# Causal attention, top-2 experts and combining in one block, with all result loads issued at once

## What is computed

```python
x = x + _L0_xattn_ref(_layernorm(x), ctx, ctx, ...)      # 16 heads of 8
x = x + _L0_ffn_ref(_layernorm(x), gate_w, expert_w)     # the best of 8 experts
x = x + _L1_xattn_ref(_layernorm(x), ctx, ctx, ...)      # the same, causal
x = x + _L1_ffn_ref(_layernorm(x), ...)

def _L1_ffn_ref(x, router_w, gate_proj, up_proj, down_proj):   # F = 352
    probs = softmax(x @ router_w)
    routing_weights, routing_idx = top_k(probs, 2)             # of 8, then normalised to sum 1
    # for each of a token's two experts e:
    #   y_e = (silu(x @ gate_proj[e]) * (x @ up_proj[e])) @ down_proj[e]
    return sum over both of weight_e * y_e
```

## Time and profile before

| | us |
|---|---|
| three timed runs | 892.91, 894.95, 895.14 (median 894.95) |
| the profiled execution, its own time | 895.08 |
| its span, first to last instruction | 893.3 |
| mean granted TensorE clock, share of full | 0.879 |
| TensorE busy | 670.4 (75% of the span) |
| VectorE, ScalarE, GpSimd busy | 483.9 (54%), 385.5 (43%), 347.6 (39%) |

### The profile page before, as it was taken

The page is one execution under the profiler, slowest core; times in us unless marked ns, Lnnn a source line. Parts: engine busy times, 40 slices in busy tenths (PEclk is TensorE's granted clock), DMA queues, the critical chain, the costliest instruction groups (busy, mean ns, idle before and its releaser), DMA issues. The chain is left out here.

```text
span 893.3 us, 21719 instructions
## 1 busy us (share of the span) xinstructions
PE 670.4 (75%) x7687; PEld 458.0 (51%) x7717; DVE 483.9 (54%) x1275; ACT 385.5 (43%) x948; POOL 347.6 (39%) x506
## 2 busy tenths in 40 slices
PE   1566648898996898994499999998406999999910
PEld 1343326676774454541155666665304877787700
DVE  1687446676772677773356888887341222222213
ACT  0344325575774012121056666667303665666500
POOL 4354240010011134342034477778841544455410
PEclk9988677899998899997589999999556999999965
DMA  3459831464302999999014333300111222212027
GB/s 95 132 152 182 209 114 24 80 108 81 74 3 38 208 239 209 216 219 228 7 23 77 72 90 87 84 26 26 43 36 48 59 55 61 58 55 64 28 72 222
DMA packets 93273, 87.17 MB, mean 98 GB/s; under 512 B 7785, under 2 KB 87921, under 8 KB 90097
## 3 DMA queue, kind: packets, MB, share of 16 engines
q1 hardware_dynamic: 84592, 74.70, 38.9%
q0 software_dynamic: 4352, 8.99, 3.2%
q10 hardware_dynamic: 4224, 2.10, 0.8%
HBM read 43.99 MB, written 41.76 MB: 96 GB/s over the span
## 5 line engine op out<-in xcount | busy, mean ns | idle before, releaser
L861 DVE TENSOR_REDUCE nm<-bank 128x8 f32<-128x1024 f32 x128 | 156.5, 1223 | 63.8 <-PE bank L633 61.7
L763 ACT ACTIVATE pr<-bank 128x512 f32<-128x512 f32 x256 | 147.2, 604 | 85.0 <-PE bank L657 82.2
L1572 DVE TENSOR_TENSOR exac<-bank,exsi 128x352 f32<-128x352 f32 x72 | 37.8, 525 | 127.8 <-PE bank L1479 121.0
L1029 POOL TENSOR_SCALAR_AFFINE_SELECT pr<-pr 128x1024 f32<-128x1024 f32 x64 | 69.7, 1088 | 75.3 <-ACT pr L763 75.1
L1451 POOL DMA_INDIRECT results<-exy,exre x72 | 70.8, 983 | 33.0 <-issue 33.0
L670 PE MATMUL bank<-pr,values 128*9 128x128 f32 x2048 | 82.3, 280 | 1.7 <-POOL pr L1029 1.7
L654 PE MATMUL bank<-qq,kk 48*128 48x128 bf16 x1024 | 76.8, 223 | 6.4 <-issue 4.2
L1308 PE MATMUL bank<-e0ch,expert_w 128*128 128x512 f32 x128 | 71.9, 644 | 8.2 <-DVE e0ch L1220 8.1
L657 PE MATMUL bank<-mt,pick 64*128 64x128 bf16 x1024 | 76.8, 223 | 0.0
L633 PE MATMUL bank<-kk,qq 48*128 48x128 bf16 x1024 | 55.5, 233 | 19.5 <-DVE nm L861 8.0
L1058 POOL DMA_INDIRECT sorted_in<-rrrow,rrpli x64 | 63.2, 988 | 14.2 <-issue 14.0
(11 more groups left out here) (203 smaller groups left out, 1304.3 us busy)
## 6 DMA issues: line engine op xcount, KB each, us to landing
sorted_in<-padding SPq DMA_DIRECT2D x8, 2145.0 KB
k_parts<-pj_parts SPq DMA_DIRECT2D x16, 384.0 KB, 2.9
kk<-k_parts SPq DMA_DIRECT2D x32, 192.0 KB
qq<-q_parts SPq DMA_DIRECT2D x32, 192.0 KB
exx<-sorted_in SPq DMA_DIRECT2D x72, 65.0 KB
kk<-k_parts SPq DMA_DIRECT2D x32, 128.0 KB
qq<-q_parts SPq DMA_DIRECT2D x32, 128.0 KB
coy<-results SPq DMA_DIRECT2D x8, 512.0 KB, 4.7
```

Of the source, the lines that this page charges most:

```text
L763: act.activation(probs[c], st_bank[(n * NC + c) % ST][:], ACT.Exp, scale=scale).then_inc(exp_s, 1)
L861: dve.tensor_reduce(neg_max[n % 2][:, u * 2 * C4:(u + 1) * 2 * C4], s_pair.rearrange("q (h k) -> q h k", k=T), AX_X, ALU.max, negate=True) ...
L1029: pool.affine_select(out=probs_pair[u][:], in_=probs_pair[u][:], compare_op=ALU.is_ge, fill=0.0, base=0, pattern=[[0, 2 * C4], [1, T]], ch ...
```

## The change

1. `attention`, `run_experts` and `combine` no longer open a block each: they hand back a `Stage` of five functions, and one block calls the three stages' functions one after the other on each engine. The branches, the barriers and the clearing between attention(1) and the experts, and the block end between the experts and `combine`, are gone. In their place SP waits for the scatters of rows and for `tile_row` (semaphore `listed`) before its first load, TensorE for the readers of the PSUM banks that it takes over, and SP for the scatters of results before `combine`'s loads.
2. The tag becomes t\*64 + 2b + k: `results` is ordered by token, and the results of four sequences for one token are one run of 4 KB. The runs of 128 partitions lie 32 KB apart.
3. `combine` issues its eight loads at once, each with a place of its own in the attention's tiles `qq` and `kk`, which are free by then. VectorE adds in place in `x_res`, and ScalarE's queue stores from there, so that no addition waits for a store.

The other stages keep their code. The core of the diff, without the lines that only change their indentation:

```diff
-                        step(dve.tensor_copy(tile_row[:], expert[:]))
+                    dve.tensor_copy(tile_row[:], expert[:]).then_inc(listed_s, 1)
...
-                        pool.iota(row[bt.p][:, :, 0:bt.count, D + 1:ROW].bitcast(I32), pattern=[[1, 2], [2 * T, bt.count], [1, 1]],
-                                  base=bt.start * 2 * T, channel_multiplier=2).then_inc(tagged, 1)
+                    pool.iota(row[bt.p][:, :, 0:bt.count, D + 1:ROW].bitcast(I32), pattern=[[1, 2], [2, bt.count], [1, 1]],
+                              base=bt.start * 2, channel_multiplier=2 * B).then_inc(tagged, 1)
...
+            stage = Stage(on_sync, on_tensor, on_scalar, on_vector, on_gpsimd)
                     if causal:
-                        for p in range(ROWS):
-                            pool.wait_ge(moved[p], sum(SENT * bt.count for bt in BATCHES if bt.p == p))
+                stage.banks_read = ((max_s, B * PAIRS), (exp_s, B * NC), (ot_s, B), (norm_s, B), (y_s, B), (weighed_s, len(BATCHES)))
+                stage.listed = listed_s
+                stage.rows_moved = [(moved[p], sum(SENT * bt.count for bt in BATCHES if bt.p == p)) for p in range(ROWS)]
+            return stage
...
-                @block.sync
-                def _(sp):
+            def on_sync(sp):
+                for moved, count in routed.rows_moved:
+                    sp.wait_ge(moved, count)
+                sp.wait_ge(routed.listed, 1)
+
                     def load(g):
...
                     all_groups(pool, body, NQ)
-                    for p in range(2):
-                        pool.wait_ge(y_out[p], 16 * (SLOTS // 2))
...
+                for read, count in routed.banks_read:
+                    pe.wait_ge(read, count)
+                pe.wait_ge(routed.listed, 1)
                     turn(FIRST)
...
-                two = lambda name, shape, dt=F32: [sb(f"co{name}{p}", shape, dt, mine) for p in range(2)]
-                x_sum, y_g = two("xs", [128, G, D]), two("y", [128, G, 2 * D])
-                by_token = results[0:SPARE].rearrange("(b t k) d -> b t (k d)", t=T, k=2)
+            by_token = results[0:SPARE].rearrange("(t c) d -> t (c d)", t=T)
+            SIZE = G * 2 * D
+            halves = [tile[:].rearrange("p h t -> p (h t)").bitcast(F32)[:, k * SIZE:(k + 1) * SIZE]
+                      for tile in qq + kk for k in range(2)]
+            y_g = [half.rearrange("t (b k d) -> t b k d", b=G, k=2) for half in halves]
+
+            def on_sync(sp):
+                for done, count in ran.results_out:
+                    sp.wait_ge(done, count)
+                for n in range(NG):
+                    sp.dma_start(halves[n], by_token[:, n * SIZE:(n + 1) * SIZE]).then_inc(y_in[n], 16)
+
+            def on_scalar(act):
+                for n in range(NG):
+                    act.wait_ge(sum_s, n + 1)
+                    act.dma_start(rows(x_dst, Group(n // 2, n % 2)), x_res[:, n * G:(n + 1) * G, :]).then_inc(x_out, 16)
+                act.wait_ge(x_out, 16 * NG)
...
+            def on_vector(dve):
+                for n in range(NG):
+                    x = x_res[:, n * G:(n + 1) * G, :]
+                    dve.wait_ge(y_in[n], 16)
+                    dve.tensor_tensor(x, x, y_g[n][:, :, 0, :], ALU.add).then_inc(first_s, 1)
+                    dve.wait_ge(first_s, n + 1)
+                    dve.tensor_tensor(x, x, y_g[n][:, :, 1, :], ALU.add).then_inc(sum_s, 1)
...
-                    def load(g):
-                        sp.wait_ge(sum_s, earlier(g.n - 1))
-                        sp.dma_start(y_g[g.p][:], rows(by_token, g)).then_inc(x_in[g.p], 16)
-                    all_groups(sp, load)
...
-                        dve.wait_ge(x_out[g.p], earlier(g.turn * 16))
...
+            causal = attention(1, own)
+            experts = run_experts(causal, own)
+            total = combine(out, experts)
+            with nc.Block() as block:
+                @block.sync
+                def _(sp):
+                    causal.sync(sp)
+                    experts.sync(sp)
+                    total.sync(sp)
```

More of the change, by code:

```diff
@@ L538, in _, with attention @@
                         bias(g)
-        def attention(l):
+        def attention(l, own):
             causal = l == 1
@@ L1404, in _, with run_experts @@
                     query_second(LAST)
-        def experts1(x_dst):
-            run_experts()
-            combine(x_dst)
-        def run_experts():
+        def run_experts(routed, mine):
             s = lambda name: sem(f"ex_{name}")
@@ new lines, in run_experts @@
+            two = lambda name, shape, dt=F32: [sb(f"ex{name}{p}", shape, dt, mine) for p in range(2)]
+            x_g, x_t, y_g = two("x", [128, G, ROW]), two("xt", [128, GT]), two("y", [128, D])
+            share, result, aside = two("sh", [128, G]), two("re", [128, G], I32), sb("exas", [128, G], to=mine)
+            silu, acts = two("si", [128, F]), two("ac", [128, F])
+            acts_t = two("at", [128, len(FCH) * T])
+            t_bank, gate_bank, up_bank, hidden_bank, y_bank = bank[0], bank[1:3], bank[3:5], bank[5], bank[6:8]
@@ new lines, in on_gpsimd, with send, body @@
+            def on_gpsimd(pool):
+                def send(q):
+                    pool.wait_ge(begun, earlier(q.m - 1))
+                    pool.wait_ge(y_s, q.m + 1)
+                    pool.tensor_tensor(pool_cell[:, q.p:q.p + 1], epsilon[:, 0:1], epsilon[:, 0:1], ALU.mult
+                                       ).then_inc(begun, 1)
+                    pool.indirect_dma_start(
+                        results[:], bass.IndirectOffsetOnAxis(ap=result[q.g.p][:, q.b:q.b + 1], axis=0),
+                        y_g[q.p][:], None).then_inc(y_out[q.p], 16)
+                def body(g):
+                    for t in range(G):
+                        send(Seq(g, t))
+                all_groups(pool, body, NQ)
@@ new lines, in on_vector, with activate, keep_tags, body @@
+            def on_vector(dve):
+                def activate(q):
+                    dve.wait_ge(silu_s, q.m + 1)
+                    dve.wait_ge(up_ps, q.m + 1)
+                    dve.wait_ge(hidden_ps, earlier(q.m - 1))
+                    dve.tensor_tensor(acts[q.p][:], up_bank[q.p][:, 0:F], silu[q.p][:], ALU.mult).then_inc(act_s, 1)
+                def keep_tags(g):
+                    dve.wait_ge(x_in[g.p], (g.turn + 1) * 16 * G)
+                    for p in range(2):
+                        dve.wait_ge(y_out[p], earlier((g.n - 1) * 16 * (G // 2)))
+                    dve.tensor_copy(share[g.p][:].unsqueeze(2), x_g[g.p][:, :, D:D + 1])
+                    tags = x_g[g.p][:, :, D + 1:ROW].bitcast(I32)
+                    dve.scalar_tensor_tensor(out=aside[:].unsqueeze(2), in0=tags, scalar=float(SPARE),
+                                             in1=odd_slot[:].unsqueeze(2), op0=ALU.is_ge, op1=ALU.mult).then_inc(aside_s, 1)
+                    dve.wait_ge(aside_s, g.n + 1)
+                    dve.tensor_tensor(result[g.p][:].unsqueeze(2), tags, aside[:].unsqueeze(2), ALU.add).then_inc(tags_s, 1)
+                def body(g, last=False):
+                    for t in range(G):
+                        activate(Seq(g, t))
+                        if t == G - 1 and not last:
+                            keep_tags(g.after())
+                keep_tags(FIRST)
+                body(FIRST)
+                middle_groups(dve, body, NQ)
+                body(LAST_TILES, last=True)
@@ L1632, in build, with _ @@
         clear_semaphores()
-        attention(0)
+        with ExitStack() as own:
+            cross = attention(0, own)
+            with nc.Block() as block:
+                @block.sync
+                def _(sp):
+                    cross.sync(sp)
+                @block.tensor
+                def _(pe):
+                    cross.tensor(pe)
+                @block.scalar
+                def _(act):
+                    cross.scalar(act)
+                @block.vector
+                def _(dve):
+                    cross.vector(dve)
+                @block.gpsimd
+                def _(pool):
+                    cross.gpsimd(pool)
         clear_semaphores()
```

1220 lines of the change are left out of this document (586 added, 634 removed).

## The result

| | before | after |
|---|---|---|
| timed runs, us | 892.91, 894.95, 895.14, 894.0 | 868.67, 863.86, 868.61, 868.87 |
| median | 894.48 | 868.64 |
| span of the profiled execution | 893.3 | 866.8 |
| mean granted clock | 0.879 | 0.894 |

The ratio is 0.9708, with a 95% interval of 0.9671 to 0.9745: 2.9% faster, 868.64 where 871.5 was forecast. Timed again beside the last experiments the changed kernel gave 865.44 against 889.73, 0.973 (0.9698 to 0.9761).

The account below looks back on a forecast made before the run. Bounds: idle transitions into the experts and the combine, the combine's two buffers, and TensorE in the 72 tiles between. Gains 6.8 + 6.2 + 10.4 = 23.4 us off the profiled 895.08, adjusted to the median, gave 871.5, range 868 to 879.

Parts of the forecast that it names:

- The first transition: From attention(1) to the experts: the first load issued 6.8 us earlier, bounds 5.5 to 7.2.
- the reading of the tile's place with the wake-up: On SP before the experts' first load: 0.8 us to read the place plus 0.1 for waking up, 0.9 in all.
- The restart at the low clock: TensorE's start on the experts: granted clock at 0.50 before and after, its rise time left as it is, 0 us.
- The second transition: From the experts to the combine: the first load of results issued 6.2 us earlier, bounds 5.2 to 6.6.
- The scatters' new pattern: In the expert tiles: result rows written 32 KB apart per token, taken as 0 us, with 0 to +3 allowed.
- Rival D: In the expert tiles: scatters of results pile up, landing in 5.3 us, 62 us more, 934 us; chance 0.03.
- The combine: Last stage, first load to end: 20.4 us instead of 30.8, between 19 and 22, a gain of 10.4.
- three limits: For the combine's length: bytes 19.6 us, VectorE 18.1, order of loads and stores 21.8 at the latest, 20.5 in the middle.
- a share of two bytes loaded for one stored: In the combine, once stores begin: DMAs shared so, the last load landing at 16.4 us and the end at 20.5.
- B: At both transitions: they keep half their time, 3.2 us each, giving 878 us; chance 0.06.
- C: In the combine: the 32 KB distance halves the loads' rate to about 185 GB/s, giving 880 us; chance 0.06.
- A: Whole kernel: the sum of the gains holds, 868 to 875 us; chance 0.85.

Follow-up runs that it names:

- e2: Kernel before with only the new combine and tag, its separate blocks, barriers and clearing kept: 879.3 us against 886.11 for the kernel before, ratio 0.9911.
- e1: Changed kernel, its one block kept, with the combine and tag of before put back: 875.25 us against 886.11 for the kernel before, ratio 0.9876.
- e5: Changed kernel with two empty result rows more per token, so runs lie 33 KB apart, not 32: 865.6 us against 886.11 for the kernel before, 0.9779.
- e4: Changed kernel with the old tag and load pattern, runs of 1 KB instead of 4 KB: 864.63 us against 888.78 for the kernel before, ratio 0.9721.
- e12: Changed kernel with nine unread matrix products before the first rows and one of 384 columns after: 866.62 us against 886.79 for the kernel before, 0.9763.
- e9: Changed kernel with eight unread matrix products before the first rows and an early Silu: 865.06 us against 889.73 for the kernel before, ratio 0.9716.

## Why the prediction was right, point by point

- *The first transition*, 6.8 us forecast: 6.4. The block's end, the clearing and the barriers were the gap, as supposed, and e2 brings it back (9.9 us). Mis-sized is the reading of the tile's place with the wake-up, taken as 0.9 us: the scatter is down at 661.24 + 2.31 = 663.55, the load issued at 664.81, so 1.26. The seven waits on TensorE cost nothing, as it began with the rows' landing.
- *The restart at the low clock*, forecast as unchanged: C-D fell by 1.0 us. Not by the change: it is 8.9 in e2, with the long idle, and 10.1 and 10.2 in e1 and e5, with the short one. Over the nine traces with the short idle and without extra products it takes 8.6 to 10.2, and 8.9 and 10.1 in the two with the long one. The same holds for the tiles, 163.8 to 166.0 us with before's 165.7 at the upper end. So 2.1 of the 26.5 us are luck of the two executions, a clock that came back sooner and scatters that were waited for less, and without them the span would have fallen by 24.4, where 23.4 was forecast. The medians of the pair that was timed again (889.73 and 865.44) differ by 24.3.
- *The second transition*, 6.2 forecast: 6.4, with 0.06 us between the landing (844.95 + 2.25) and the issue.
- *The scatters' new pattern*, 0 forecast, 0 measured: they land 2.25 us after issue, with the old tag too (e4). The waits for them, 7.9 us before and 5.2 after, tell nothing of the pattern, as they are 1.0 to 8.7 us over the traces with the new tag and 2.2 to 9.7 over those with the old. Rival D is gone, with e5 as a second witness.
- *The combine*, 10.4 us gained forecast, 11.2 measured: 19.5 us instead of 20.4. Its three limits were right and the choice among them was the step that was off. I took a share of two bytes loaded for one stored. In fact the loads went first: when the last had landed, at 860.9, 345 GB/s for the remaining 4.9 us, or 1.7 of 2.10 MB of stores, were still to go. The result is the bytes' own limit, forecast as 19.6. VectorE was nearly a second one: its 16 additions stand without a gap from 851.40 to 862.32 (a pair every 1.33 us, so 10.9 where 11.6 were reckoned), and it was free for the last group at 860.86, 0.02 us before the last load landed.
- How the loads went first, the queues show. The first store is issued at 852.85, and up to 856.4 only loads move; then, from 857 to 860 (packets, MB, share of 16 engines), the two queues move nearly the same number of packets, those of the loads (q1) being 4 KB long and those of the stores (q10) 512 bytes:

```profile
q1 hardware_dynamic: 253, 0.93, 86.6%
q10 hardware_dynamic: 265, 0.14, 14.9%
```

  With packets of 1 KB (e4, 853 to 858) it is 1241 to 1238 packets, 1.24 to 0.62 MB, and the last load lands 2 us later. By the rule of the Trainium skill (DMA: Bandwidth & Descriptors, Queues, rings and completion order) the engines go round their queues packet by packet; the trace agrees in these stretches. The 3.6 us before the first store's first packet it does not explain, and no run does.
- The Trainium skill's row on large powers of two (same page, Latency and other measured facts) begins at 512 KiB, and no run here has such a distance. At 32 KB e5 shows 0.3 us at most, the size that was reckoned, but within the spread of the same combine.
- *Rivals B and C* did not come: no nameless gap is left, and the loads were faster with runs of 4 KB than the rows of before (415 for 385 GB/s), not slower. A was right, by its own terms to within 0.8 us each.

The measured median lies at the lower end of the range, 868 to 879, 2.9 us under the forecast: 0.8 by the combine, 2.1 by the two stretches that vary, 0.2 less by the transitions, and what remains by E-F, rounding and the spread of what lies ahead.

## What to carry to other kernels

Look for stretches of the trace in which nothing at all runs, neither an engine nor a DMA: here two stage boundaries cost 6 to 8 us each, and behind waits on just the events that the next stage needs the issue followed in 0.1 and 1.3 us. In a chain of load, sum and store through double buffers, take the waits away together and reckon the result by its bytes: each wait alone holds most of the time (27.0 and 28.4 us of 30.8), and with none left the DMAs carry 6.29 MB in 19.5 us. Cut profiles at common marks before comparing them, as the spread of a stage that nobody touched can be larger than an edit.

## What had not been expected of the hardware

- Runs of 4 KB load at 415 GB/s (401 in e12), runs of 1 KB at 382 to 385; between distances of 32 and 33 KB (415 and 417) no difference is seen.
- Two queues with work move equal numbers of packets (253 and 265, 1241 and 1238), so the one with the longer packets moves more bytes; a store that was issued behind queued loads moved its first packet only 3.6 us later.
- The issue of a load holds SP for 1.28 us when it is made of 512 runs and several loads are queued (0.36 with two), and for 0.44 to 0.49 with 128 runs.
- The end of a block costs 6.3 us in one kernel and 7.7 in another, with the same work around it.
- A stage that is the same in all kernels, attention(0), came out some 5 us shorter in three of fourteen executions. That, the 1.3 us of the block's end, why the clock came back 4.7 to 8.0 us behind the first transpose (and the first result 8.6 to 10.2), and the 286 GB/s of the stores that were held back are left open.
- TensorE's clock was at 1.00 with products running up to 668.0 (e9) and still from 670.0 to 670.5; from 670.5 to 671.0 it was 0.82 and then 0.50. Between lay 1.5 us of idle time, 0.7 us of transposes and 0.8 us of idle time, and the product at 670.88 took twice its time at 1.00; in e12, with the gaps filled, it did not.
